# First attention: the queries turned once, and the turned row maxima put into them by transfers

## The reference

```python
q = _apply_rope((x @ Wq).reshape(b, t, 32, 16).transpose(0, 2, 1, 3), cos, sin)
k = _apply_rope((x @ Wk).reshape(b, t, 8, 16).transpose(0, 2, 1, 3), cos, sin)
scores = jnp.einsum('bhqd,bhkd->bhqk', q, repeat(k, 4)) / math.sqrt(16)
scores = jnp.where(causal, finfo.min, scores)
attn = jax.nn.softmax(scores, axis=-1)          # exp(score - row maximum), divided by the row sum
ctx = jnp.einsum('bhqk,bhkd->bhqd', attn, repeat(v, 4))
return ctx.transpose(0, 2, 1, 3).reshape(b, t, 512) @ Wo
```

## Time and profile before

| | |
|---|---|
| three timed executions | 1361.17, 1360.54, 1359.83 us; median 1360.54 us |
| profiled execution, first to last instruction (span) | 1357.2 us |
| busy over the span | PE 97%, PE weight loads 78%, DVE 76%, POOL 52%, ACT 53% |
| the attention of the change | about 57 us to 320 us of the span |
| transfers issued by SP in that stretch | 2 at its start, 4 at 245 us, 2 from 289 us |
| granted TensorE clock | 0.998 of full speed, mean |

### The profile page before, as it was taken

One profiled execution on the slowest core, in us unless ns is written; L12 is line 12 of the kernel. 1 busy time (PEld: TensorE's weight loads), 2 busy tenths in 40 slices (PEclk: granted clock), 3 DMA queues, 4 the chain that ended last, 5 costly groups with the idle time before them and its releaser, 6 DMA issues. The chain is left out here.

```text
span 1357.2 us, 20247 instructions
## 1 busy us (share of the span) xinstructions
PE 1320.4 (97%) x6683; PEld 1055.9 (78%) x6683; DVE 1036.8 (76%) x2438; ACT 721.1 (53%) x1558; POOL 712.1 (52%) x641
## 2 busy tenths in 40 slices
PE   8899999998999999999999999999999999899999
PEld 6666667755776788888888888888888888688877
DVE  8888888876678887787787778777877878775553
ACT  3488887784454544454445545444544455443433
POOL 5589997773646443542444344335424433256643
PEclk9999999999999999999999999999999999999999
DMA  4000000101102110110111101101101001112222
GB/s 147 1 1 1 2 1 2 32 17 55 40 1 78 32 39 9 39 40 17 32 32 31 33 16 32 40 8 35 45 17 32 24 3 46 29 45 59 66 69 84
DMA packets 53335, 45.08 MB, mean 33 GB/s; under 512 B 4400, under 2 KB 42672, under 8 KB 52976
## 3 DMA queue, kind: packets, MB, share of 16 engines
q1 hardware_dynamic: 53232, 43.79, 10.9%
HBM read 41.69 MB, written 2.10 MB: 32 GB/s over the span
## 5 line engine op out<-in xcount | busy, mean ns | idle before, releaser
L1973 POOL TENSOR_TENSOR a_p_lo<-a_prob,a_p_hi 128x512 fp32r<-128x512 f32 x160 | 202.9, 1293 | 21.4 <-ACT a_p_hi L1817 20.7
L244 DVE CUSTOM_DVE_ANT_0 a_score<-a_score,mask_w 128x384 f32<-128x384 f32 (+3 forms) x384 | 196.6, 558 | 9.7 <-PE a_score L1396 7.0
L738 ACT ACTIVATE a_pt_hi<-a_ring 128x512 fp32r<-128x512 f32 x160 | 93.9, 597 | 161.8 <-PE a_ring L422 161.8
L896 POOL TENSOR_TENSOR a_rot_a<-a_rot_a,a_rot_b 128x512 f32<-128x512 f32 x79 | 102.3, 1295 | 146.5 <-DVE a_rot_b L600 146.5
L729 ACT ACTIVATE a_prob<-a_score,a_nmax 128x128 f32<-128x128 f32 (+3 forms) x256 | 132.0, 529 | 57.9 <-DVE a_nmax L244 57.8
L365 PE MATMUL a_xo<-h_hi,w_both 128*128 128x512 f32 x384 | 150.5, 392 | 1.8 <-DVE a_rot_b L600 1.4
L367 PE MATMUL a_xo<-h_hi,w_both 128*128 128x512 f32 x384 | 150.2, 391 | 0.0
L366 PE MATMUL a_xo<-h_lo,w_both 128*128 128x512 f32 x384 | 149.5, 389 | 0.0
L901 POOL TENSOR_TENSOR a_p_lo<-a_rot_a,a_p_hi 128x512 fp32r<-128x512 f32 x79 | 102.3, 1296 | 65.7 <-ACT a_p_hi L755 65.7
L580 DVE TENSOR_TENSOR a_pt_lo<-a_ring,a_pt_hi 128x512 fp32r<-128x512 f32 x160 | 108.6, 687 | 32.1 <-ACT a_pt_hi L738 31.1
L574 DVE TENSOR_SCALAR a_prob<-a_prob,a_rinv 128x128 f32<-128x128 f32 (+3 forms) x256 | 107.8, 464 | 4.8
(11 more groups left out here) (424 smaller groups left out, 3655.0 us busy)
## 6 DMA issues: line engine op xcount, KB each, us to landing
raw<-in_L_attn_wq SPq DMA_DIRECT2D x32, 256.0 KB, 2.9
raw<-in_L_attn_wo SPq DMA_DIRECT2D x32, 256.0 KB, 2.6
raw<-in_L_gate_up_t SPq DMA_DIRECT2D x20, 256.0 KB, 3.1
raw<-in_L_down_t SPq DMA_DIRECT2D x20, 256.0 KB, 3.0
raw<-in_L_attn_wk SPq DMA_DIRECT2D x8, 256.0 KB, 2.9
raw<-in_L_attn_wv SPq DMA_DIRECT2D x8, 256.0 KB, 2.9
out<-x SPq DMA_DIRECT2D x8, 256.0 KB, 2.5
x<-in_L_attn_x SPq DMA_DIRECT2D x3, 512.0 KB, 8.6
```

The lines of the kernel that those rows point to most:

```text
L244: return nc.vector.tensor_tensor_reduce(scores, scores, m.mask_w[:, T - n:T], -1.0, LARGE, ALU.add, ALU.min, to)
L896: nc.gpsimd.tensor_tensor(of_a, of_a, of_b, ALU.add).then_inc(summed, 1)
L1973: nc.gpsimd.tensor_tensor(p_lo[:, mm % NP, :], prob[:, mm % NE, :], p_hi[:, mm % NP, :].bitcast(F32), ALU.subtract).then_inc(p_ready, 1)
```

## The change

The second turn of the queries is gone, and so are `put_maxima` on POOL, the ring `q_max` and DVE's copy into it. `q_rows` becomes a ring of four. PE turns only the 8 columns of row maxima of a tile (one transpose instead of four, `turn_maxima`), DVE splits the turned 8x128 block into its high and low part in `mx` (two dependent instructions, `split_maxima`), and SP puts them with 8 transfers (4 heads by high and low, two rows of 512 bytes each) into the two last-group rows of each key head in `q_rows`. `turned_scores` reads `q_rows` once all 8 have landed.

PE's list: `turn_maxima(u, 0)`, `(u, 1)` and `(u, 3)` stand where the second turns stood; `turn_maxima(u, 2)` stands before `scores(u, 3, 0, 3)` instead of behind `turned_scores(u, 1, 1, 0)`; `turned_scores(u-1, 3, 0, 0)` moves behind `turn_queries(u, 1)` and the two `scores(u, 0, ...)`. DVE's list: `split_maxima` stands where `read_queries` stood, but that of tile 2 one place and `read_heads(u-1, 3)` earlier, before `maxima(u, 3, 0, 3)`. `c_hi` and `c_lo` shrink from two tiles to one. SP issues the low-rank weights before the transfers of (7, 0), and the gate and up weights before those of (7, 3).

```diff
-        q_rows, q_max = sb("q_rows", [P, HPG, P], F32R), sb("q_max", [P, NQ, HPG, P], F32R)
-        nmax = sb("nmax", [P, 2, HPG, X2])
+        q_rows = sb("q_rows", [P, NQ, HPG, P], F32R)
+        nmax, mx = sb("nmax", [P, 2, X2, HPG]), sb("mx", [P, 2, 2, P], F32R)
...
+        max_put = [sem(f"max_put{k}") for k in range(2)]
+        MAX_PUT = 16 * 2 * HPG
...
+            for n in range(QT * NU):
+                if n == QT * (PAIRS + 3):
+                    sp.wait_ge(c_turned, QT)
+                    for g in range(4):
+                        sp.dma_start(b_raw[32 * g:32 * (g + 1), :], inp["L0_b13e"]).then_inc(m.b_loaded, 16)
+                if n == QT * NU - 1:
+                    sp.wait_ge(q_turned, QT * NU)
+                    for part in range(2):
+                        load_gate_up_part(sp, m, inp, part, m.w_loaded[part])
+                sp.wait_ge(mx_read, n + 1)
+                for h in range(HPG):
+                    for e in range(2):
+                        sp.dma_start(q_rows[48 + e:P:64, n % NQ, h, :].bitcast(F32),
+                                     mx[h:X2 * HPG:HPG, n % 2, e, :].bitcast(F32)).then_inc(max_put[n % 2], 16)
...
+            def turn_maxima(u, i):
...
+                pe.wait_ge(score_read, scored_by[n])
+                claim_qkbank(mx_read, n + 1)
+                nc.tensor.transpose(qkbank[0:X2 * HPG, 0:P], nmax[:, i % 2, :, :].rearrange("p x h -> p (x h)"),
+                                    m.ident[:, :]).then_inc(qm_turned, 1)
...
                 if x == 0 and j == 0:
-                    pe.wait_ge(qm_read, QT * u + i + 1)
+                    pe.wait_ge(max_put[i % 2], MAX_PUT * ((QT * u + i) // 2 + 1))
...
-            def read_queries(u, i):
+            def split_maxima(u, i):
...
                 dve.wait_ge(qm_turned, n + 1)
...
+                if n >= 2:
+                    dve.wait_ge(max_put[n % 2], MAX_PUT * (n // 2))
+                hi = mx[0:rows, n % 2, 0, :]
+                nc.vector.tensor_copy(hi, qkbank[0:rows, 0:P]).then_inc(mx_hi, 1)
+                dve.wait_ge(mx_hi, n + 1)
+                nc.vector.tensor_tensor(mx[0:rows, n % 2, 1, :], qkbank[0:rows, 0:P], hi.bitcast(F32),
+                                        ALU.subtract).then_inc(mx_read, 1)
...
-                nc.gpsimd.tensor_copy(heads[:, :, 0], both).then_inc(parted, 1)
-                pool.wait_ge(parted, 2 * n + 1)
-                nc.gpsimd.tensor_tensor(heads[:, :, 1], both, heads[:, :, 0].bitcast(F32), ALU.subtract).then_inc(parted, 1)
```

More of the change, by code:

```diff
@@ L1258, in attend0 @@
     NS = 3
-    NE, NP, NQ = 3, 4, 2
+    NE, NP, NQ = 3, 4, 4
     V1 = HD0 + 1
@@ L1287, in attend0 @@
         head = m.head
-        c_hi, c_lo = sb("c_hi", [P, 2, KT, P], F32R), sb("c_lo", [P, 2, KT, P], F32R)
+        c_hi, c_lo = sb("c_hi", [P, KT, P], F32R), sb("c_lo", [P, KT, P], F32R)
         score = [ps(f"score{k}") for k in range(NS)]
@@ L1307, in attend0 @@
             "keys_turned", "q_turned", "qm_turned", "scored", "t_scored", "weighed", "backed", "c_turned", "projected"))
-        keys_read, qm_read, score_read, parted, c_read, divided, head_ready, c_ready = (sem(n) for n in (
-            "keys_read", "qm_read", "score_read", "parted", "c_read", "divided", "head_ready", "c_ready"))
+        keys_read, mx_hi, mx_read, score_read, c_read, divided, head_ready, c_ready = (sem(n) for n in (
+            "keys_read", "mx_hi", "mx_read", "score_read", "c_read", "divided", "head_ready", "c_ready"))
+        max_put = [sem(f"max_put{k}") for k in range(2)]
+        MAX_PUT = 16 * 2 * HPG
         q_read, exped, p_hi_done, p_ready, c_hi_done = (sem(n) for n in (
@@ L1361, in turn_keys, with turn_queries @@
                 last.then_inc(keys_turned, 1)
-            def turn_queries(u, i, again):
+            def turn_queries(u, i):
                 if not live(u):
@@ L1376, in turn_queries @@
                     last = nc.tensor.transpose(qkbank[:, r * P:(r + 1) * P], x.rearrange("p x s n -> p (x s n)"), m.ident[:, :])
-                last.then_inc(qm_turned if again else q_turned, 1)
+                last.then_inc(q_turned, 1)
+            def turn_maxima(u, i):
+                if not live(u):
+                    return
+                n = QT * u + i
+                pe.wait_ge(score_read, scored_by[n])
+                claim_qkbank(mx_read, n + 1)
+                nc.tensor.transpose(qkbank[0:X2 * HPG, 0:P], nmax[:, i % 2, :, :].rearrange("p x h -> p (x h)"),
+                                    m.ident[:, :]).then_inc(qm_turned, 1)
             def scores(u, i, x, bank):
@@ L1395, in scores @@
                 if per == 1:
-                    nc.tensor.matmul(out[:, 0:n], q_rows[:, bank, :], k_rows[:, u % 2, x, 0:n], start=True,
+                    nc.tensor.matmul(out[:, 0:n], q_rows[:, (QT * u + i) % NQ, bank, :], k_rows[:, u % 2, x, 0:n], start=True,
                                      stop=True).then_inc(scored, 1)
@@ L1402, in scores @@
                     to = out[:, X2 * h * n:X2 * (h + 1) * n].rearrange("p (x n) -> p x n", x=X2)
-                    nc.tensor.matmul(to, q_rows[:, first + h, :], k_rows[:, u % 2, 0:X2, 0:n], start=(h == 0), stop=False)
+                    nc.tensor.matmul(to, q_rows[:, (QT * u + i) % NQ, first + h, :], k_rows[:, u % 2, 0:X2, 0:n], start=(h == 0), stop=False)
                 diagonal = out[:, 0:per * n].rearrange("p (h n) -> p h n", h=per)[:, :, i * P:n]
@@ L1417, in turned_scores @@
                 out = turned[mm % 2][:, :].rearrange("p (h n) -> p h n", h=HPG)
-                last = nc.tensor.matmul(out, k_rows[:, u % 2, x, j * P:(j + 1) * P], q_max[:, (QT * u + i) % NQ, :, :],
+                last = nc.tensor.matmul(out, k_rows[:, u % 2, x, j * P:(j + 1) * P], q_rows[:, (QT * u + i) % NQ, :, :],
                                         start=True, stop=(j < i))
@@ L1465, in project_tile @@
                 for k in range(KT):
-                    nc.tensor.matmul(out[:, :], c_hi[:, t % 2, k, :], wo_hi[:, k, :], start=(k == 0), stop=False)
-                    high = nc.tensor.matmul(out[:, :], c_hi[:, t % 2, k, :], wo_lo[:, k, :], start=False, stop=False)
-                    last = nc.tensor.matmul(out[:, :], c_lo[:, t % 2, k, :], wo_hi[:, k, :], start=False, stop=(k == KT - 1))
+                    nc.tensor.matmul(out[:, :], c_hi[:, k, :], wo_hi[:, k, :], start=(k == 0), stop=False)
+                    high = nc.tensor.matmul(out[:, :], c_hi[:, k, :], wo_lo[:, k, :], start=False, stop=False)
+                    last = nc.tensor.matmul(out[:, :], c_lo[:, k, :], wo_hi[:, k, :], start=False, stop=(k == KT - 1))
                 high.then_inc(projected, 1)
@@ L1484, in _ @@
                 tail = u == NU
-                turn_queries(u - 1, 3, 1)
+                turn_maxima(u - 1, 3)
                 weigh(u - 1, 1, 1, 1)
@@ L1496, in _ @@
                     turn_tile(QT)
-                turned_scores(u - 1, 3, 0, 0)
-                turn_queries(u, 1, 0)
+                turn_queries(u, 1)
                 scores(u, 0, 0, 0)
                 scores(u, 0, 1, 0)
+                turned_scores(u - 1, 3, 0, 0)
                 turned_scores(u - 1, 3, 1, 0)
@@ L1506, in _ @@
                 weigh(u - 1, 2, 1, 2)
-                turn_queries(u, 0, 1)
+                turn_maxima(u, 0)
                 turned_scores(u - 1, 3, 1, 1)
@@ L1515, in _ @@
                 scores(u, 1, 1, 1)
-                turn_queries(u, 2, 0)
+                turn_queries(u, 2)
                 turn_back(u - 1, 2)
@@ L1530, in _ @@
                 turned_scores(u - 1, 3, 1, 3)
-                turn_queries(u, 1, 1)
+                turn_maxima(u, 1)
                 weigh(u - 1, 3, 1, 1)
@@ L1539, in _ @@
                 turned_scores(u, 0, 0, 0)
-                turn_queries(u, 3, 0)
+                turn_queries(u, 3)
                 scores(u, 2, 1, 3)
@@ L1553, in _ @@
                 scores(u, 3, 0, 2)
+                turn_maxima(u, 2)
                 scores(u, 3, 0, 3)
@@ L1573, in _ @@
                 scores(u, 3, 1, 3)
-                turn_queries(u + 1, 0, 0)
+                turn_queries(u + 1, 0)
                 if first is not None:
@@ L1608, in maxima @@
                         dve.wait_ge(zeroed, 3)
-                    masked_maximum(nc, m, next_score(), n, nmax[:, i % 2, bank, x:x + 1]).then_inc(score_read, 1)
+                    masked_maximum(nc, m, next_score(), n, nmax[:, i % 2, x, bank:bank + 1]).then_inc(score_read, 1)
                     return
-                at = (x * S_BANKS[i] + bank) * per
-                nc.vector.tensor_reduce(nmax[:, i % 2, :, :].rearrange("p h x -> p (h x)")[:, at:at + per],
-                                        next_score()[:, 0:per * n].rearrange("p (h n) -> p h n", h=per),
+                heads = per // X2
+                first = (x * S_BANKS[i] + bank) * heads
+                nc.vector.tensor_reduce(nmax[:, i % 2, :, first:first + heads].rearrange("p x h -> p h x"),
```

(31 more changed lines are left out.)

11 lines of the change are left out of this document (3 added, 8 removed).

## The result

The changed kernel takes 1411.04 us (median, 1408.46 to 1413.51); beside it the kernel before takes 1360.56. The ratio is 1.0376, with a 95% interval of 1.0364 to 1.0388: 50 us slower. The forecast was 1387, its range 1356 to 1408.

A forecast was written before the change was run, and what follows sets the result against it. POOL (busy 29.36 of 30 us) and PE were both taken to set the pace. Six ordinary units at +3.8 us and two projection units at +1.9 gave +26.6 us, from 1360.5 to 1387 us; range 1356 to 1408.

The forecast's parts named there:

- SP's wake-up: On SP, after DVE's split and before the first put is issued: 0.05 us.
- rival of cheap issue: Issuing two-row puts on SP is cheap: gain below a 0.17 us step, 1347 us from about 0.08; chance 0.16.
- rival of transfers holding each other up: Two engines carry all 8 puts in turn, or slower landing and step: 5.35 us and more, 1404 us and above; chance 0.13.
- chain behind the split: From DVE's split to the landing of the eighth put: 4.6 us, bounds by rows 4.05 to 5.35.
- window by window: Chain against PE's time from turn_maxima to turned scores: tile 1 +2.0, tile 2 +2.3, tile 3 +0.2 us, ordinary unit.
- other waits: PE's 0.8 us a unit of waiting, such as for ACT; half goes since POOL is no longer late.
- What is removed: POOL loses 1.8 us and PE 1.0 us a unit; with nothing added, 13 us faster.
- 25.2 of POOL's own work: POOL's work in us per ordinary unit after the removal, to which the unit would fall were nothing added.
- SP issues 8 transfers: On SP, a step of 0.38 us per put, the last of 8 issued 2.7 us after the first.
- The last one lands: From the eighth put's issue to its landing in q_rows: 1.9 us, between rows of 1.7 and 2.3.
- The split itself: DVE's two dependent small instructions on the turned maxima: 0.6 us, bounds 0.4 to 0.7.
- DVE's arrival: From PE's turn of the maxima to DVE's split: 0.8, 0.85, about 0.9 and 0.36 us for tiles 0 to 3.

The follow-up runs named there:

- no puts: All 256 puts left out of the changed kernel, turned scores waiting for DVE's split alone, maxima missing: 1360.42 us, ratio 0.9994.
- busy waits: The changed kernel with dummy matmuls on PE ahead of the wait for the puts, before tiles 1, 2 and 3: 1406.68 us, ratio 1.0339.

## Why the prediction was right in sign and wrong in size

The mechanism was right: PE waits for the landing of the eighth put, before tiles 1 and 2 most, before tile 3 little, in projection units not before tile 1; POOL ceases to be the bound. The 0.05 us for SP's wake-up is 0.03 in the trace. The rival of cheap issue is refuted by the 0.52 us a step. The prediction tried a step of 50 ns from the Trainium skill ("DMA: Bandwidth & Descriptors", Anatomy of one DMA). That section breaks down a transfer issued by GpSimd, and its 50 ns is the sequencer's dispatch alone. For SP's issues this trace shows 0.52 us. The fixed 2 us of the same section is nearer to the 1.5 us from the last issue to the end of PE's wait. The rival of transfers holding each other up is refuted too: the landing is 1.5 us behind four and behind eight. But the chain behind the split, 5.1 to 5.4 us, is nearly the 5.35 of that rival: by the prediction's own sum it makes 1399 to 1405 us, still inside the range. What put the time outside is the gain that didn't come and the clock.

The sum missed 24 of 50 us. With the kernels above as its steps:

| term | in the prediction | measured |
|---|---|---|
| removed work, moves included | 6 x 1.44 + 2 x 1.04 = -11 | no puts against before: -0.2 |
| waits for the puts | 6 x 5.3 + 2 x 3.0 = +38 | busy waits against no puts: +46.3 |
| clock after the waits | none | changed kernel against busy waits: +4.4 |
| sum | +27 | +50.5 |

(In the prediction the two upper terms stand netted, window by window; 1.44 is four times 0.26 and the 0.4 of other waits, 5.3 the waits of tiles 1 to 3 against windows shortened by 0.26 each.)

**What is removed** is the step that failed, and the largest miss. It held that the freed time of PE falls to the sum wherever no put is waited for, and that half of PE's other waits goes as well. With the puts left out, -0.2 us stood where the sum had -11. Two causes are shown by runs. The prediction looked at the buffers (`c_hi`, `c_lo`) and at the windows, and not at the bank: the moved `turn_maxima(u, 2)` needs `qkbank` while DVE still makes the context's low part from it, 1.09 us in each projection unit, and moving the turn back removed just that. The move of `turned_scores(u-1, 3, 0, 0)` was priced as 0.23 us shifted from one window to the next; it makes ACT wait 0.77 and POOL 0.49, and undoing it, with the turn already back, shortened the unit from 26.67 to 26.2, about 0.45 us. And even with both undone, a unit is 26.2 us, not the 25.2 of POOL's own work: the removed work is worth 5 us, not the 11 of the sum or the 13 that I gave for a change with nothing added. The 25.2 could not have come by the prediction's own count either: it had the steps of PE at 26.3, less 1.0 is 25.3, with the waits on top. And those waits did not halve. What PE's weight loads wait for, 60 to 320 us, in the kernel before (the earlier trace rows has 8.3 us in 18 for ACT)

```profile
PEld a_score L1396 <- DVE a_nmax L244: 4.3, 14, 0.7
```

and with the puts left out and both moves undone:

```profile
PEld a_turned L1431 <- ACT a_prob L1825: 8.6, 24, 1.1
PEld a_score L1409 <- DVE a_nmax L244: 7.9, 22, 1.0
```

The waits for ACT stay, those for DVE's maxima grow, and the projection units (33.1 and 33.7, before 33.6) gain 0.2 us on average instead of 1.0. How much of the 26.2 these waits explain is not settled: a weight load can wait while PE still works, and PE is busy 29.96 of 30 by modelled ends, which can't tell a full PE from one that stops briefly and often. The single `c_hi` was not tested by itself; it stays in every kernel here.

**SP issues 8 transfers.** A step of 0.38 was taken; it was 0.52. The 0.38 is the step behind the 8 KB transfer, the first of its pair; the smallest, of 1 KB, lasted 0.42 itself, which with the 0.05 between two makes a step of 0.47. The four loads of 256 KB start 0.38, 0.47 and 0.46 apart, and not 0.43 each. The trace of before had still longer steps outside the attention, which the prediction did not look at, such as 8.12 - 7.58 = 0.54 for 16 KB:

```profile
7.58 0.49 SPq L1047 DMA_DIRECT2D mask_w<-in_c_sin  x1
8.12 0.55 SPq L1047 DMA_DIRECT2D mask_w<-in_c_nsin  x1
```

So the upper bound of 0.43 was too low by rows of before, whatever the shape of the puts. **The last one lands** in 1.5 us, not 1.9. Together 5.1 to 5.4 us behind the split instead of 4.6; three chains in an ordinary unit and two in a projection unit give 6 x 3 x 0.6 + 2 x 2 x 0.6 = 13 by that, and 8 were measured; the difference is open. The split itself, 0.58 us, and DVE's arrival, 172.44 - 171.56 = 0.88 for tile 1, were right.

**The clock** had no term. I knew it at 1.00 in every stretch of before and did not ask what idle stretches of 3 us would do to it.

## What to carry to other kernels

A small transfer cost its issuer about half a microsecond here whether it carried 1 KB or 4 KB: before splitting a move over a loop of transfers, write it as few wide ones, then count (N - 1) steps and one landing into the dependent engine's wait. Take the step from issues that follow one another, over the whole trace, and not from the first of a pair. Test a removal by itself, with what replaces it left out: it shows at once whether the gain that is to pay for the new wait exists. When a step is moved, look at the bank it needs at its new place, and at which engine would have been fed by what now stands behind it.

## What the runs showed of the hardware

- SP's step from one SBUF to SBUF transfer to the next: 0.52 us for 2 rows of 512 bytes, 0.54 for 8 rows (two issues last 1.03, one 0.495), 0.62 for four pieces of 512 bytes into one row. Four loads of 256 KB started 0.38, 0.47 and 0.46 apart, so small ones are not the cheaper ones. In the kernel before, an issue behind a pause lasts 0.33 and 0.34 us (at 58.09 and 245.15), the ones right behind it 0.42 each.
- From the issue of the last transfer to PE's matmul it is 1.5 us (two rows), 1.6 (eight rows) or 1.7 (one row), behind four issues as behind eight. Four of the waits ended only after 2.1 to 2.5 us; why is open.
- After PE had been idle for 2.9 us its granted clock was 0.50 in the next 3 us and 0.95 in the 3 after; with dummy matmuls in the wait it stayed at 1.00 in the profiled execution.
